# Every fourth gate tile's low half moves from DVE to POOL

## The reference, cut to what matters

```python
x = x + 0.5 * _L0_ffn_ref(_layernorm(x, axis=-1), gate_w, w1, w2, w3)   # layer 0 of experts
x = x + _L0_attn_ref(_layernorm(x, axis=-1), W_q, W_k, gain, bias, log_mix, log_scale)
x = x + 0.5 * _L0_ffn_ref(_layernorm(x, axis=-1), gate_w, w1, w2, w3)   # layer 1 of experts

# in _L0_ffn_ref: two of eight experts for each of 4096 tokens
probs = softmax(xf @ gate_w.T);  weights, idx = top_k(probs, 2)
x1 = silu(einsum('td,efd->tef', xf, w1));  x3 = einsum('td,efd->tef', xf, w3)
out_all = einsum('tef,edf->ted', x1 * x3, w2)          # 256 -> 512 -> 256
```

## Time and profile before

| | us |
|---|---|
| median of 3 runs | 791.7 (789.98 to 792.04) |
| profiled execution, its own time | 792.64 |
| its span, first to last instruction | 791.1 |
| PE busy in the span | 689.9 |
| DVE busy | 555.1 |
| ACT busy | 497.8 |
| POOL busy | 455.5 |

### The profile page before, as it was taken

One profiled execution on the slowest core, in us unless ns is written; L12 is line 12 of the kernel. 1 busy time (PEld: TensorE's weight loads), 2 busy tenths in 40 slices (PEclk: granted clock), 3 DMA queues, 4 the chain that ended last, 5 costly groups with the idle time before them and its releaser, 6 DMA issues.

```text
span 791.1 us, 17293 instructions
## 1 busy us (share of the span) xinstructions
PE 689.9 (87%) x4632; PEld 427.3 (54%) x4632; DVE 555.1 (70%) x1535; ACT 497.8 (63%) x927; POOL 455.5 (58%) x545
## 2 busy tenths in 40 slices
PE   1741658999999999999999999999999999999992
PEld 1730225566556565665565656655665655565652
DVE  6789862433787888888988898888865624333866
ACT  4667633453568886968889788977876334343441
POOL 3477878644434457467576745774776756341442
PEclk9975789999999999999999999999999999999997
DMA  9985486888796989888989899788989989778999
GB/s 335 428 276 142 131 234 162 160 141 154 178 194 114 197 150 166 186 168 180 167 183 197 167 186 174 149 183 140 189 159 184 186 187 165 133 155 190 261 244 326
DMA packets 318613, 150.74 MB, mean 191 GB/s; under 512 B 299133, under 2 KB 302589, under 8 KB 317757
## 3 DMA queue, kind: packets, MB, share of 16 engines
q1 hardware_dynamic: 300637, 111.98, 69.3%
q0 software_dynamic: 17888, 37.65, 17.3%
HBM read 33.96 MB, written 44.81 MB: 100 GB/s over the span
## 4 chain that ended last, share of the span: by engine, by line
PE 43%; DMA 11%; DVE 10%; issue 6%; SPq 5%; ACT 4%; POOL 4%; POOLq 1%; ACTq 0%; DVEq 0%
PE B L1263 25%; PE B L1279 14%; DMA t_W<-t_W 2%; DMA t_gh<-t_gp 2%; DVE t_X L1794 2%; PE B L1292 2%; SPq L1124 1%; SPq L1068 1%; DMA t_ph<-t_p 1%; PE B L1306 1%; DMA t_hp<-yt 1%; DVE t_gp L1785 1%; DVE t_th L1774 1%; PE B L1331 1%; SPq L1084 1%
## 5 line engine op out<-in xcount | busy, mean ns | idle before, releaser
L1263 PE MATMUL B<-t_W,t_ht 128*128 x1704 | 398.0, 383 | 23.0 <-DVE t_th L1774 11.5
L1263 PEld LDWEIGHTS B<-t_W,t_ht 128*128 128x128 f16 x1704 | 166.5, 98 | 202.1 <-issue 37.3
L1774 DVE SCALAR_TENSOR_TENSOR t_th<-B,t_K,t_th 128x512 f32<-128x512 f32 x142 | 105.6, 747 | 110.6 <-PE B L1263 101.2
L1024 POOL DMA_INDIRECT yt<-t_W,t_idx x104 | 111.1, 1068 | 115.7 <-ACT t_W L1424 72.5
L1279 PE MATMUL B<-t_W,t_gh 128*128 x1284 | 157.3, 273 | 6.3 <-ACT t_W L1424 3.6
L976 POOL DMA_INDIRECT hs<-t_s,t_POS x112 | 117.7, 1050 | 58.2 <-issue 28.6
L1406 ACT ACTIVATE t_th<-B,t_K 128x512 f32<-128x512 f32 x142 | 96.9, 683 | 76.6 <-PE B L1263 71.0
L1279 PEld LDWEIGHTS B<-t_W,t_gh 128*128 128x128 f16 x1284 | 123.8, 98 | 38.5 <-issue 10.1
L1785 DVE TENSOR_TENSOR t_gp<-t_th,t_gp 128x512 f16<-128x512 f32 x107 | 75.4, 711 | 26.9 <-ACT t_gp L1415 26.7
L1415 ACT ACTIVATE t_gp<-t_th 128x512 f16<-128x512 f32 x107 | 66.3, 624 | 40.3 <-DVE t_th L1774 35.4
L1016 POOL DMA_DIRECT2D t_idx<-hs x142 | 80.2, 570 | 17.8 <-DMA yt<-t_W,t_idx 8.5
(11 more groups left out here) (216 smaller groups left out, 897.1 us busy)
## 6 DMA issues: line engine op xcount, KB each, us to landing
t_W<-wk SPq DMA_DIRECT2D x6, 2048.0 KB, 24.9
t_hp<-yt SPq DMA_DIRECT2D x16, 512.0 KB
t_s<-yt SPq DMA_DIRECT2D x15, 512.0 KB, 5.6
t_X<-x SPq DMA_DIRECT2D x8, 512.0 KB, 7.2
out<-t_X SPq DMA_DIRECT2D x7, 512.0 KB, 4.9
t_ht<-hs SPq DMA_TRANSPOSE x142
t_idx<-hs POOLq DMA_DIRECT2D x142, 0.5 KB, 3.3
hs<-t_ph SPq DMA_DIRECT2D x2, 952.0 KB, 5.3
```

The source lines that it names most:

```text
L1024: eng.indirect_dma_start(yt_d[L], bass.IndirectOffsetOnAxis(ap=IDX[:, n % RING:n % RING + 1], axis=0), yout(n), None).then_inc(d_y[n % YR] ...
L1263: t = eng.matmul(B[b][:], HT[n % HTR][:, (2 * hl + db) * 128:(2 * hl + db) * 128 + 128], W16[:, bass.ds(expert[n] * 4096 + (db * 2048 + wl ...
L1774: eng.scalar_tensor_tensor(out=th[:], in0=B[b1][:], scalar=K[:, 7:8], in1=th[:], op0=ALU.mult, op1=ALU.mult).then_inc(free[b1], 1)
```

## The change

For the 19 tiles n = 23, 27, ..., 95 the instruction glow(n) is issued by POOL, in the place that glow has in ORDER, with the same operands. It counts on a semaphore of its own, s_gq; whoever waited for the glow (gt on SP, tanh(n+3) on ACT) waits on s_gq for these tiles and on s_gl, which now counts the other 123, for the rest.

```diff
+        def on_pool(n):
+
+            return 20 <= n < 96 and n % 4 == 3
+
+        def lowered(n):
+
+            same = [m for m in range(n + 1) if on_pool(m) == on_pool(n)]
+            return s_gq if on_pool(n) else s_gl, len(same)
...
+                elif kind == "glow" and on_pool(key[0]):
+                    n, = key
+                    th, gp = TH[n % THR], GP[n % LAG]
+                    e.wait_ge(s_gh, n + 1)
+                    eng.tensor_tensor(gp[:, 1, :], th[:], gp[:, 0, :], ALU.subtract).then_inc(s_gq, 1)
...
                 elif kind == "gt":
                     n, = key
-                    e.wait_ge(s_gl, n + 1)
+                    e.wait_ge(*lowered(n))
...
                     if n >= THR:
-                        e.wait_ge(s_gl, n - THR + 1)
+                        e.wait_ge(*lowered(n - THR))
                     eng.activation(TH[n % THR][:], B[b][:], ACT.Silu, scale=K[:, 0:1]).then_inc(free[b], 1)
...
                 elif kind == "glow":
                     n, = key
-                    th, gp = TH[n % THR], GP[n % LAG]
-                    e.wait_ge(s_gh, n + 1)
-                    eng.tensor_tensor(gp[:, 1, :], th[:], gp[:, 0, :], ALU.subtract).then_inc(s_gl, 1)
+                    if not on_pool(n):
+                        th, gp = TH[n % THR], GP[n % LAG]
+                        e.wait_ge(s_gh, n + 1)
+                        eng.tensor_tensor(gp[:, 1, :], th[:], gp[:, 0, :], ALU.subtract).then_inc(s_gl, 1)
```

More of the change, by code:

```diff
@@ L771, in macaron_kernel @@
         s_gl = sem("s_gl")
+        s_gq = sem("s_gq")
         s_y = sem("s_y")
@@ L1197, in _ @@
                     flat = B[b][:, :].bitcast(F16)
-                    e.wait_ge(s_gl if h else s_gh, n + 1)
+                    if h:
+                        e.wait_ge(*lowered(n))
+                    else:
+                        e.wait_ge(s_gh, n + 1)
                     e.wait_ge(free[b], turn)
```

## The result

The changed kernel takes 808.7 us in the median (806.35 to 814.17, 6 runs); the kernel before, run beside it, 790.84 us (787.16 to 794.11). The ratio is 1.0225 with a 95% interval of 1.02 to 1.0251: 17.9 us slower, where 4.4 us were forecast. The profiled executions, 808.82 us with a span of 807.3 us after, 792.64 and 791.1 us before, are 16.2 us apart.

What follows compares the result with a forecast made beforehand. PE was taken to set the pace. Losses of 7.9 us at three tiles, less 2.0 taken up and 1.5 of DVE's relief, gave +4.4 us: 796.1 us, range 788.8 to 800.2.

Steps and rivals of the forecast that it cites:

- The price of a glow on POOL: Each 128x512 subtraction on POOL was to take 1.3 us, with 0.8 to 1.6 us as the ends.
- Tile 55: Glow behind ids(64) delays the table load and tanh(58) on ACT; PE loses 4.4 us ahead of up(59,1).
- Tile 67: Glow behind the last of eight scatters delays the transpose that down(67) needs; PE loses 3.0 us.
- Tile 83: Glow behind root(15) ends at 534.8, after ACT's table load for tanh(86) had gone; PE loses 0.5 us.
- Taken up: After tile 67, PE's later idle time up to 610 us was to absorb 2.0 us of the losses.
- Sixteen come out free: All changed tiles but 55, 67 and 83 were to cost nothing, POOL being ready and otherwise idle while blocked.
- What the reads cost DVE: 24.7 us more POOL arithmetic reading SBUF was to stretch DVE's instructions by 3.7 us.
- What PE sees of DVE's relief: With DVE relieved by 10.3 us, PE was to gain 1.5 us, half of its 3.2 us of waits for DVE.
- PE idle in 190 to 610 us: PE's idle time in the stretch holding all 19 tiles was to rise from 16.0 to about 20 us.
- the third rival: POOL's reads block DVE for each full 1.3 us: +9.5, 801.2 us; a clock fall would look alike; chance 0.13.
- the absorbed loss: Rival: idle time takes up losses of tiles 67 and 83 and half of 55: +0.7, 792.4 us; chance 0.22.
- the winning relief: Rival: gates free banks earlier, PE's waits shrink and POOL reaches tile 55 in time: 787.7 us; chance 0.15.

Runs made afterwards that it cites:

- second profiled execution: The changed kernel run once more, unchanged, on another chip beside the kernel before: 811.87 us, 1.0259.
- hold: Kernel before, DVE computing all glows, but POOL waits at the 19 places for the high half and runs nothing there: 798.17 us, 1.0069.
- hold_read: Kernel before plus, at the 19 places, POOL's wait for the high half and two 128x192 subtractions reading SBUF into an unused buffer: 818.81 us, 1.0173.
- hold_write: Kernel before plus, at the 19 places, POOL's wait for the high half and four 128x192 memsets, which read nothing: 803.72 us, 1.016.
- placed: Changed kernel with all 19 glows on POOL, ten of them elsewhere in POOL's order: 806.65 us, 1.0059 of the kernel before.
- only55: Kernel before with only the glow of tile 55 moved to POOL, in the changed kernel's place: 807.32 us, 1.0066.
- late3: Kernel before with only the glows of tiles 87, 91 and 95 moved to POOL: 806.76 us, 1.0073.
- late3_placed: Kernel before with only glows 87, 91 and 95 on POOL, 87 behind put(83) and 91 behind affine(7,0): 796.63 us, 1.0036.

## Why the prediction was wrong in size

The direction and the first mechanism were right; the sum was a quarter of the loss. By its steps:

- **The price of a glow on POOL**, 1.3 us: measured 1.17. Right.
- **Tile 55**, 4.4 us: the chain is the one forecast, PE's wait 4.13 us. The lag settles 3.6 us higher; alone it costs 5.3 us (2.6 to 8.0 by its interval). The chain is right. That the sum is near is in part luck: "Tile 55 I count in full" leaves out the fall of the clock, which adds to it (lag up to 10.05), and a wait of PE of 1.84 us for another DMA, there before at 396.8 us and gone after, which takes some of it up (lag down to 8.40).
- **Tile 67**, 3.0 us: the lag rises by 2.1 us by down(68), but PE's wait for the transpose itself is only 0.40 us; 0.71 us ahead of it is a wait for DVE, and 1.00 us at 464.3 us one for another DMA. The size is near, the chain is not the one forecast. **Tile 83**, 0.5 us: PE waits 1.84 us where it waited 1.00, 0.8 us more. **Taken up**, 2.0 us: 1.4 us after tile 67 and 1.3 between down(94) and down(110). Tiles 55, 67 and 83 alone cost 0.4%, 3.2 us.
- **"Sixteen come out free: POOL's turn is there soon enough, and the time in which the glow blocks POOL is idle time."** This step failed. The sixteen alone cost 1.12%, 9.0 us. The prediction asked whether the glow would be late for its own readers; it did not follow what stands behind the glow in POOL's queue up to PE, except at tiles 39 and 67. At 39 it was right: the glow waited 5.43 us for high(39), and the first five tiles cost nothing that can be told. At 87, 91 and 95 the steps behind were scatters and an affine that ACT's queue, and through it PE's evict, were waiting for: 2.7 us of lag at 87 and 3.6 at 91 and 95 (with a fall of the clock), and 0.73% for these three alone.
- **What the reads cost DVE**, 3.7 us: measured 15.7 us (557.6 against 541.9 busy; 13.7 in the second profiled execution). The prediction took the excess of the mean over the median of one group and doubled it. Of the 15.7 us only 2.6 are in the glows left on DVE; 2.2 are in 64 instructions of line 1813, 2.0 in 16 steps of 128x4, and 1.5 each in two groups of 16 routing steps of 128x32, by the same groups of the kernel before; the estimate had only a guess for all of these. "DVE busy down by about 10 us" came out as 2.5 us more, over the span and over the same matmuls alike.
- **What PE sees of DVE's relief**, 1.5 us (at most 3.2): the whole work taken away gives 3.0 us (0.2 to 5.8), which does not tell 1.5 from 3.2. But the change does not get it, as the point above says; in the lag 0.8 us of it is seen.
- **PE idle in 190 to 610 us**, forecast about 20: measured 24.9 in that stretch and 26.0 over the same matmuls.
- **The clock** stood in the third rival, as something that would come out in the same region. It fell three times, 3.4 us each, about 5 us of the loss, and the forecast had no term for it. This is the second step that failed.

Of the rivals, the absorbed loss and the winning relief are out. The third had both of its mechanisms happen, blocked reads on DVE and a fall of the clock, and came nearest in size (801.2 us); yet its cause is not the main one: waiting in POOL's queue plus POOL's time costs 1.6% without any read, and moving ten glows takes away some 1.7 to 2.0% with all reads kept.

An account of the whole from runs beside before: waiting alone 0.7%; POOL occupied at the same places 0.9% on top, with the falls of the clock that came with it; the late hand-over at tile 55 (which hold, hold_read and hold_write do not have) 0.66%; together 2.3%, against 2.25 and 2.6% measured. That they add up is an assumption, since tiles 55, 67 and 83 and the other sixteen did not (1.5%). Not settled: what the same waits would cost if the clock did not fall, since no run took the two apart (the trace gives only what the falls added, 5.4 us); what reads cost in the placed kernel, where the remaining 0.6% may be POOL's time or DVE's stretch; and the 1.87 us of lag ahead of tile 23, which the change cannot have made (0.98 us in the second profiled execution).

## What to carry to other kernels

Moving work to an idle engine adds two things to that engine's queue, its time and the wait for its operand: price both for every step behind it, up to the engine that bounds the kernel, at each place and not by the busy share. The bare wait can be tried alone, and here it showed places that were wrong before anything was computed. And subtract from the relief what two engines that read the same memory take from each other.

## What the runs showed of the hardware

- POOL's subtraction of 128x512, float32 minus float16, takes 1173 ns where its 128x256 instructions take 801 and 811: 1.46 times for twice the columns.
- 22.3 us of such POOL instructions stretched DVE's by 13.7 to 15.7 us in all, while 24.6 us of POOL subtractions on float16 operands stretched it by 6.1 (561.2 against 555.1) and 19.9 us of memsets by nothing (553.4). Why the float16 ones cost less than half was not looked into. A 128x32 DVE step went from 0.19 to 1.14 us.
- Such 128x32 comparisons and products of float32 in SBUF, taken from all 17 traces: 191 to 195 ns with no POOL instruction beside them (336 of them), at most 267 ns beside POOL's DMA issues alone (346), 191 to 192 ns beside its memsets (4), but 501 ns in the median and up to 1145 ns beside its two-input arithmetic alone (123). DVE's gates, with one operand in PSUM, did not move: 746 ns after, 747 before.
- PE's clock was at 1.2 GHz for 3.4 or 6.8 us at a time. It fell inside or right behind waits of PE of 4.30 us (only55, from 380.9 us on), 4.13, 2.80 and 2.37 us (the kernel after), 2.22 us (late3) and 2.10 us (late3_placed). It is not a matter of the wait's length alone: behind 2.39 us at tile 87, in the kernel after and in hold alike, and behind 2.10 us in placed, it did not fall.
